# Gathers of a mixture-of-experts stage issued by two engines in turn instead of by one

## The chip, the cores and the metric

The kernel runs on 1 core of one Trainium2 chip. The metric is the device time of one execution in microseconds (us). The engines are TensorE (PE in the profile, with PEld for its weight loads), VectorE (DVE), ScalarE (ACT), GpSimd (POOL) and the sequencer SyncE (SP), which computes nothing and issues transfers. Sixteen DMA engines carry every transfer, whichever engine issued it.

## The reference, cut to what matters

```
x: (32, 256, 256), adj: (256, 256)
x = x + attention(layernorm(x), adj)           # 8 heads, masked softmax
h = layernorm(x)                               # 8192 rows of 256, in groups of 16 rows
grouped = h.reshape(B, S // 16, 16, D)
logits = einsum('bgtd,des->bgtes', grouped, controller) + tie
perm = (logits == max(logits over t))          # each of 64 experts picks one row of each group
inter = einsum('bgtesf,bgtes->bgesf', einsum('bgtd,desf->bgtesf', grouped, f1), perm)
inter2 = einsum('bgesf,esfd->bgesd', relu(inter), f2)
x = x + einsum('bgesd,bgtes->bgtd', inter2, perm)
```

The change is in the last two lines: the experts' products must come back from an order by expert to an order by group, and are then scattered to the rows.

## The kernel before, in words

Everything is float32. The first two thirds of the span are the attention, batch by batch. The rest is the mixture stage, of which this document speaks. It handles 64 tiles of 128 rows in 4 chunks (`CHUNKS`, `c` 0 to 3) of 16 tiles (`CT`). A chunk has two stages.

**Units.** Four units (`u` 0 to 3) of four tiles each (`t` 0 to 3). In program order TensorE does, for unit `u`: the transposes of the unit two ahead (L546), `select` of tile 0 (L650), the one-hot transposes of the next unit (L566), `select` of tile 1, the logits of the unit two ahead (L559), `select` of tiles 2 and 3. Each `select` leaves its result in four PSUM banks, which VectorE and ScalarE copy to `XS` (L246, half each), and the next `select` waits for both halves (`sel_dve`, `sel_act`). ScalarE's list for a unit is: copy of the transposes (`save_h2T`, L774, two copies), `save_selected` 0, copy of the one-hot matrix (`save_one_hot`, L779), `save_selected` 1, 2, 3. In chunk 3 the last two units have nothing ahead, so units 2 and 3 have no `save_h2T`, and unit 3 has no `save_one_hot`.

**Experts.** For 16 quads of experts: expand (L661), relu, contract (L682), a copy of the products to one of 5 slots of `stage` (L918 on ScalarE, L1246 on VectorE), and `move` (L325 on SP), a transfer of 512 KB from that slot to the DRAM tensor `scratch`. Each slot has its semaphore in `moved`.

**Gathers.** When all moves of chunk `c` have landed, 16 gathers (L335, on SP) bring `scratch` back by expert, one for each tile, 512 KB each, into the same 5 slots, now called `XR`: tile `i` goes to slot `i % 5`. They run beside the units of chunk `c + 1`, where TensorE does 8 scatters (L709) of two tiles each, between the selects: units 1, 2 and 3 have scatters 0 to 2, 3 to 5, and 6 and 7. The scatter after select 0 (and the one-hot transposes) comes first, then one after select 2, then one after select 3; unit 3 has only the first two. Scatter `s` needs tiles `2s` and `2s + 1` landed (`gathered`) and the result of scatter `s - 1` added by VectorE (`finish`, L1204). A gather of tile 5 or more waits until the scatter that read its slot is done:

```
                elif tile >= SLOTS:
                    sp.wait_ge(sc_ready, c * (CT // 2) + (tile - SLOTS) // 2 + 1)
```

So tiles 5 and 6 wait for scatter 0, 7 and 8 for scatter 1, 9 and 10 for scatter 2, 11 and 12 for scatter 3, 13 and 14 for scatter 4, and 15 for scatter 5. After the gathers SP stores the finished rows (L341, 8 transfers of 256 KB).

**Tail.** After the experts of chunk 3 there are no units. Four gathers of 2 MB (L356, on SP, into `XRlast`, four tiles each, semaphores `last_in`) are issued one behind the other, TensorE does two scatters (L695) for each that lands, VectorE adds them (L1204), and SP stores the rows (L341).

ScalarE issues transfers only at the very start of the kernel (weights and biases, L758 to L763); in the mixture stage it issues none.

Of the kernel before, what the change touches and what calls it, by code (L numbers as in the profile page):

```python
# [23 lines left out]
def gnn_moe_kernel(nc, x, adj, Wq, bq, Wk, bk, Wv, bv, Wo, bo, controller, f1, f2, out):  # L24
    B, N, D = x.shape
# [10 lines left out]
    CT = 16  # L36
    CHUNKS = TILES // CT
    UT = 4
    UNITS = CT // UT
    GPT = P // T  # L40
    CG = CT * GPT
    CP = CG // 2
    QUADS = ES // 4
    SLOTS = 5
# [23 lines left out]
    with ExitStack() as ctx:  # L68
# [200 lines left out]
        def products(q, hf):  # L269

            b = first_bank(q, hf)
            return stage[:, q % SLOTS, 2 * hf:2 * hf + 2, :], banks[:, b:b + 2, 0:D]

        def uses_of_slot(s):

            return (QUADS - s + SLOTS - 1) // SLOTS
# [10 lines left out]
        @block.sync  # L287
        def _(sp):
            def load_x(b, par):
                if in_loop(b) or (b - par) * 8 > 0:  # L290
                    sp.wait_ge(x_in[par], (b - par) * 8)
                sp.dma_start(xbatch(X1, b), xbatch(xt, b)).then_inc(x_in[par], 16)

            def stack_parts(b, par):

                sp.wait_ge(q_saved, b + 1)
                sp.wait_ge(k_saved, b + 1)
                for j in range(HPG):
                    src = parts[32 * j:32 * j + 32, par, :, :, :].rearrange("p s g n -> p s (g n)")
                    for r, chosen in enumerate((slice(0, 3, 2), slice(0, 4, 3), slice(1, 3, 1), slice(1, 4, 2))):  # L300
                        sp.dma_start(stack[32 * r:32 * r + 32, par, j, :, :].bitcast(F32), src[:, chosen, :].bitcast(F32))\  # L301
                            .then_inc(stacked[par][j // 2], 16)
            for b in range(6):
                load_x(b, b % 2)
                if b == 1:
                    sp.dma_start(adjs, adj.rearrange("(t p) k -> p t k", p=P)).then_inc(adj_in, 16)
            stack_parts(0, 0)
            stack_parts(1, 1)
            with sp.Fori(1, B // 2 - 2) as i:
                for par in range(2):  # L310
                    load_x(i * 2 + (4 + par), par)
                for par in range(2):
                    stack_parts(i * 2 + par, par)
            sp.dma_start(ctl[:, :, :], controller.rearrange("(t p) e s -> p t (e s)", p=P)).then_inc(ctl_in, 16)
            for b in range(B - 4, B):
                stack_parts(b, b % 2)
            sp.dma_start(f1s[:, :, :, :], f1.rearrange("(t p) e s f -> p t (e s) f", p=P)).then_inc(ffn_in, 16)
            sp.dma_start(f2s[:, :, :], f2.rearrange("e s f d -> (e s f) d").rearrange("(q p) d -> p q d", p=P))\
              .then_inc(ffn_in, 16)
            def move(c, q):  # L320

                n = c * QUADS + q
                sp.wait_ge(st_dve, n + 1)
                sp.wait_ge(st_act, n + 1)
                sp.dma_start(by_group(c, q), stage[:, q % SLOTS, :, :].rearrange("p j d -> p (j d)"))\  # L325
                    .then_inc(moved[q % SLOTS], 16)

            def gather(c, tile):

                if tile == 0:  # L330
                    for i, m in enumerate(moved):
                        sp.wait_ge(m, (c + 1) * uses_of_slot(i) * 16)
                elif tile >= SLOTS:
                    sp.wait_ge(sc_ready, c * (CT // 2) + (tile - SLOTS) // 2 + 1)
                sp.dma_start(XR[:, tile % SLOTS, :, :], by_expert(c, tile)).then_inc(gathered[tile % SLOTS], 16)  # L335

            def store(c, s):
                n = c * (CT // 2) + s
                sp.wait_ge(fin_done, n + 1)
                tiles = slice(2 * n, 2 * n + 2)  # L340
                sp.dma_start(ot[:, tiles, :], X1[:, tiles, :]).then_inc(out_done, 16)  # L341

            for c in range(CHUNKS - 1):
                for q in range(QUADS):
                    move(c, q)
                for tile in range(CT):
                    gather(c, tile)
                for s in range(CT // 2):
                    store(c, s)
            for q in range(QUADS):  # L350
                move(CHUNKS - 1, q)
            for i, m in enumerate(moved):
                sp.wait_ge(m, CHUNKS * uses_of_slot(i) * 16)
            for i in range(4):
                rows = slice((CHUNKS - 1) * CG + 4 * GPT * i, (CHUNKS - 1) * CG + 4 * GPT * (i + 1))
                sp.dma_start(XRlast[:, 4 * i:4 * i + 4, :, :].rearrange("p t j d -> p (t j) d"),  # L356
                             scratch[rows, :].rearrange("(c two) (e d) -> (two e) c d", two=2, d=D))\
                    .then_inc(last_in[i], 16)
            for s in range(CT // 2):
                store(CHUNKS - 1, s)  # L360
            sp.wait_ge(out_done, CHUNKS * (CT // 2) * 16)
# [394 lines left out]
        def _(act):  # L756
# [131 lines left out]
            def save_selected(c, u, t):  # L888
                act.wait_ge(sel_ready, c * CT + u * UT + t + 1)
                copy_selected(nc.scalar.copy, u * UT + t, 1).then_inc(sel_act, 1)  # L890

            def unit(c, u):
                n = c * UNITS + u
                ahead = n + AHEAD < CHUNKS * UNITS
                if ahead:
                    save_h2T(n + AHEAD)
                save_selected(c, u, 0)
                if n + 1 < CHUNKS * UNITS:
                    save_one_hot(n + 1)
                save_selected(c, u, 1)  # L900
                save_selected(c, u, 2)
                save_selected(c, u, 3)

            def experts(c):
                def save_inner(q):
                    act.wait_ge(in_ready, c * QUADS + q + 1)
                    if q >= INNERS:
                        act.wait_ge(f2_ready, (c * QUADS + q - INNERS) * 2 + 2)
                    nc.scalar.activation(inner[:, q % INNERS, :], bank[q % 2][:, 0:CG], ACT.Relu).then_inc(in_act, 1)
                save_inner(0)  # L910
                for q in range(QUADS):
                    if q + 1 < QUADS and (q + 1) % 2 == 0:
                        save_inner(q + 1)
                    act.wait_ge(f2_ready, (c * QUADS + q) * 2 + 2)
                    s = q % SLOTS
                    if landed(c, q) > 16:
                        act.wait_ge(moved[s], landed(c, q) - 16)
                    nc.scalar.copy(*products(q, 1)).then_inc(st_act, 1)  # L918

            for c in range(CHUNKS):  # L920
                for u in range(UNITS):
                    unit(c, u)
                experts(c)


        @block.vector
# [350 lines left out]
```

## Time and profile before

| | us |
|---|---|
| median of 3 timed runs | 808.16 (806.3 to 810.27) |
| profiled execution | 806.59 |
| its span | 804.8 |
| attention, up to the first unit | 0 to 544.3 |
| units of chunk 0 (no scatters) | 544.3 to 569.2 |
| units of chunk 1, with the gathers of chunk 0 | 591.2 to 627.7 |
| units of chunk 2, with the gathers of chunk 1 | 649.75 to 685.95 |
| units of chunk 3, with the gathers of chunk 2 | 708.0 to 743.6 |
| tail, from the last copy of products to the end | 766.4 to 804.8 |
| busy: PE 728.1, DVE 612.7, ACT 568.3, POOL 125.4 | |

Times within the kernel are microseconds from the start of the span. Between the unit stages lie the experts, 22 us each. The profiled execution is 1.8 us longer than its span and 1.6 us below the median of the timed runs.

### The profile page before, as it was taken

The numbers are of one execution on the slowest core, as the hardware profiler recorded it, in microseconds if no ns is written. First come the engines' busy times: TensorE is split into PE (matmuls) and PEld (weight loads), VectorE is DVE, ScalarE is ACT, GpSimd is POOL, SyncE is SP. The second block draws the span as 40 slices with busy tenths as digits, with TensorE's granted clock in tenths as the row PEclk, the third lists the DMA queues.
The fourth block names the chain that finished last, engine by engine and source line by source line (L and its number), as shares of the span: only waits on it lengthen the run. The fifth ranks groups of instructions, "written<-read, shape, count | busy, mean of one in ns | idle before, by whom it ended". The sixth has DMA issues, their size and how long they took to land.

```text
span 804.8 us, 22451 instructions
## 1 busy us (share of the span) xinstructions
PE 728.1 (90%) x7252; PEld 556.7 (69%) x7252; DVE 612.7 (76%) x2558; ACT 568.3 (71%) x1654; POOL 125.4 (16%) x125
## 2 busy tenths in 40 slices
PE   4789999999999999999999999897888988986925
PEld 3578888888888888888888888765554555553602
DVE  2588998998988989989989989777656656655612
ACT  3499899899999998998998999765553453442500
POOL 1100100000010010001001003436425225200000
PEclk9899999999999999999999999999999999999956
DMA  6476656756765765666567466650589889889889
GB/s 157 105 170 144 160 136 154 172 137 138 171 155 121 170 155 133 161 154 154 139 154 171 112 138 140 151 204 2 211 312 339 329 312 334 338 304 345 345 303 303
DMA packets 102197, 157.60 MB, mean 196 GB/s; under 512 B 12288, under 2 KB 65024, under 8 KB 101888
## 3 DMA queue, kind: packets, MB, share of 16 engines
q1 hardware_dynamic: 99968, 155.56, 67.7%
q10 hardware_dynamic: 2176, 1.31, 0.7%
q8 instruction: 35, 0.57, 0.3%
q14 instruction: 18, 0.15, 0.1%
HBM read 47.78 MB, written 41.94 MB: 111 GB/s over the span
## 4 chain that ended last, share of the span: by engine, by line
PE 71%; DMA 14%; SPq 6%; DVE 5%; issue 2%; ACT 1%; ACTq 0%; DVEq 0%
PE bank L501 13%; PE bank L453 12%; DMA stage<-scratch 7%; PE bank L515 7%; PE bank L488 7%; PE bank L475 6%; PE bank L682 6%; PE bank L538 6%; PE bank L661 5%; SPq L301 4%; DMA XRlast<-scratch 2%; PE bank L446 2%; DMA scratch<-stage 2%; PE bank L650 2%; PE bank L709 2%
## 5 line engine op out<-in xcount | busy, mean ns | idle before, releaser
L826 ACT ACTIVATE Ps<-Ps,nmax 128x256 f32<-128x256 f32 x512 | 255.3, 503 | 23.4 <-DVE nmax L1015 21.7
L1015 DVE CUSTOM_DVE_ANT_0 Ps<-bank,masks 128x256 f32<-128x256 f32 x512 | 199.3, 420 | 27.2 <-issue 25.4
L501 PE MATMUL bank<-ident,Ps 128*128 128x128 f32 x1024 | 145.6, 275 | 2.0 <-DVE PTs L1026 1.5
L501 PEld LDWEIGHTS bank<-ident,Ps 128*128 128x128 f32 x1024 | 115.8, 140 | 20.2 <-issue 12.4
L453 PE MATMUL bank<-hT,WT 128*128 128x256 f32 x512 | 125.2, 389 | 0.8 <-ACT hT L783 0.8
L488 PE MATMUL bank<-stack 128*128 128x256 f32 x512 | 118.0, 332 | 6.2 <-DMA stack<-parts 6.0
L382 POOL TENSOR_TENSOR X<-X,bob 128x512 f32 (+1 forms) x32 | 40.8, 1277 | 431.5 <-ACT hn L791 431.5
L453 PEld LDWEIGHTS bank<-hT,WT 128*128 128x128 f32 x512 | 95.6, 196 | 12.2 <-issue 1.1
L826 ACT ACTIVATION_READ_ACCUMULATOR Ps<-Ps,nmax 128x1 f32 x512 | 98.1, 192 | 0.0
L394 POOL TENSOR_SCALAR h<-X,mv,roots 128x256 f32<-128x256 f32 x64 | 80.1, 1263 | 113.5 <-PE bank L650 85.7
L1026 DVE COPY PTs<-bank 128x512 f32<-128x512 f32 x128 | 87.7, 685 | 4.9 <-PE bank L501 4.8
L488 PEld LDWEIGHTS bank<-stack 128*128 128x128 f32 x512 | 80.5, 191 | 14.1 <-issue 5.0
L246 ACT COPY XS<-bank 128x512 f32<-128x512 f32 x64 | 37.8, 590 | 59.9 <-PE bank L650 59.9
L835 ACT COPY PTs<-bank 128x512 f32<-128x512 f32 x128 | 73.9, 577 | 0.4 <-PE bank L501 0.4
L809 ACT ACTIVATE parts<-bank,few 128x256 fp32r<-128x256 f32 x128 | 53.7, 471 | 26.3 <-PE bank L453 24.3
L515 PE MATMUL bank<-PTs,Vs 128*32 128x256 f32 x1024 | 68.5, 385 | 0.0
L918 ACT COPY stage<-bank 128x512 f32<-128x512 f32 x64 | 37.5, 587 | 42.9 <-PE bank L682 42.9
L1001 DVE SCALAR_TENSOR_TENSOR parts<-bank,few,parts 128x256 fp32r<-128x256 f32 x128 | 58.0, 479 | 8.4 <-ACT parts L809 8.4
L246 DVE COPY XS<-bank 128x512 f32<-128x512 f32 x64 | 44.6, 697 | 26.0 <-PE bank L650 25.9
L475 PE MATMUL bank<-WT,hT 128*128 128x256 f32 x256 | 61.9, 385 | 2.0 <-DVE parts L1001 1.8
L1204 DVE TENSOR_TENSOR X<-X,bank 128x512 f32<-128x512 f32 x32 | 22.0, 688 | 54.7 <-PE bank L695 31.1
L1246 DVE COPY stage<-bank 128x512 f32<-128x512 f32 x64 | 43.9, 691 | 25.1 <-PE bank L682 25.1
(84 smaller groups left out, 1028.8 us busy)
## 6 DMA issues: line engine op xcount, KB each, us to landing
stack<-parts SPq DMA_DIRECT2D x512, 128.0 KB, 2.4
scratch<-stage SPq DMA_DIRECT2D x64, 512.0 KB, 4.0
stage<-scratch SPq DMA_DIRECT2D x48, 512.0 KB, 6.2
X<-in_x SPq DMA_DIRECT2D x32, 256.0 KB, 2.8
out<-X SPq DMA_DIRECT2D x32, 256.0 KB, 4.7
XRlast<-scratch SPq DMA_DIRECT2D x4, 2048.0 KB, 15.9
f1s<-in_L_ffn_f SPq DMA_DIRECT2D x1, 2048.0 KB, 8.0
f2s<-in_L_ffn_f SPq DMA_DIRECT2D x1, 2048.0 KB, 13.9
```

Of the source, the lines that this page charges most:

```text
L246: return copy(XS[:, :, :, first:first + 4].rearrange("p k e (j two) -> p k e j two", two=2), banks[:, 4 + 2 * hf:6 + 2 * hf, 0:2 * P].rear ...
L394: last = nc.gpsimd.tensor_scalar(h2[n % NORMS][:, t, :], xtile(tile), mv2[:, tile, 0:1], roots[:, 1, tile:tile + 1], ALU.subtract, ALU.mult)
L453: last = nc.tensor.matmul(m[:, g * N:g * N + N], WT[:, w, k, g * P:g * P + P], hT[:, k, :], start=(k == 0), stop=(k == KT - 1))
L475: last = nc.tensor.matmul(M[0][:, t * D:t * D + D], hT[:, k, t * P:t * P + P], WT[:, 2, k, :], start=(k == 0), stop=(k == KT - 1))
L488: last = nc.tensor.matmul(s_bank(n)[:, h * N:h * N + N], stack[:, par, j, 0, g * N + t * P:g * N + t * P + P], stack[:, par, j, 1, g * N:g ...
L501: last = nc.tensor.transpose(PTb[h % 2][:, k * N + t * P:k * N + t * P + P], Ps[:, pr % 2, t, h % 2, k * P:k * P + P], ident[:, :])
L515: last = nc.tensor.matmul(Ob[32 * j:32 * j + 32, g * N:g * N + N], Vs[:, par, k, h * DH:h * DH + DH], PTs[:, h, k * N:k * N + N], start=(k ...
L826: last = nc.scalar.activation(Ps[:, pr % 2, t, h, :], Ps[:, pr % 2, t, h, :], ACT.Exp, bias=nmax[:, pr % 2, t, h:h + 1], scale=-1.0, accum ...
L835: nc.scalar.copy(PTs[:, h, :], PTb[h % 2][:, :]).then_inc(pt_act, 1)
L1001: low = nc.vector.scalar_tensor_tensor(parts[:, par, 2 * which + 1, g, :], M[1 - which][:, g * N:g * N + N], (bqs, bks)[which][:, g:g + 1] ...
L1015: last = nc.vector.tensor_tensor_reduce(out=Ps[:, pr % 2, t, h, :], in0=s_bank(n)[:, h * N:h * N + N], in1=masks[:, t, :], scale=1.0, scal ...
L1026: nc.vector.tensor_copy(PTs[:, h, :], PTb[h % 2][:, :]).then_inc(pt_dve, 1)
```

## The change

Even tiles are gathered by SP as before. Odd tiles are gathered by ScalarE, on ScalarE's own queue, from within its list of the units: it waits for `moved` and issues tiles 1 and 3 in unit 0 behind `save_one_hot`, and issues the others ahead of certain `save_selected`, by a table. In the tail SP issues the first and the third 2 MB gather, and ScalarE the second and the fourth. The waits on `sc_ready` stay as they were for each tile.

```diff
@@ sync
-                for tile in range(CT):
+                for tile in range(0, CT, 2):
                     gather(c, tile)
...
-            for i in range(4):
-                rows = slice((CHUNKS - 1) * CG + 4 * GPT * i, (CHUNKS - 1) * CG + 4 * GPT * (i + 1))
-                sp.dma_start(XRlast[:, 4 * i:4 * i + 4, :, :].rearrange("p t j d -> p (t j) d"),
-                             scratch[rows, :].rearrange("(c two) (e d) -> (two e) c d", two=2, d=D))\
-                    .then_inc(last_in[i], 16)
+            for i in range(0, 4, 2):
+                sp.dma_start(*last_rows(i)).then_inc(last_in[i], 16)
@@ scalar, unit(c, u)
-                save_selected(c, u, 1)
-                save_selected(c, u, 2)
-                save_selected(c, u, 3)
+                if c > 0 and u == 0:
+                    for i, m in enumerate(moved):
+                        act.wait_ge(m, c * uses_of_slot(i) * 16)
+                    for tile in range(1, SLOTS, 2):
+                        gather(c - 1, tile)
+                after = {(1, 1): 5, (1, 3): 7, (2, 1): 9, (2, 2): 11, (2, 3): 13, (3, 1): 15}
+                for t in range(1, UT):
+                    if c > 0 and (u, t) in after:
+                        gather(c - 1, after[u, t])
+                    save_selected(c, u, t)
+
+            def gather(c, tile):
+
+                if tile >= SLOTS:
+                    act.wait_ge(sc_ready, c * (CT // 2) + (tile - SLOTS) // 2 + 1)
+                act.dma_start(XR[:, tile % SLOTS, :, :], by_expert(c, tile)).then_inc(gathered[tile % SLOTS], 16)
@@ scalar, after the last experts
+            for i, m in enumerate(moved):
+                act.wait_ge(m, CHUNKS * uses_of_slot(i) * 16)
+            for i in range(1, 4, 2):
+                act.dma_start(*last_rows(i)).then_inc(last_in[i], 16)
```

`last_rows(i)` returns the same pair of destination and source that the removed lines wrote out.

## Rows read from the trace of the kernel before

**Rows 1.** Page, the span in 40 slices: DMA share in tenths, and rate.

```profile
DMA  6476656756765765666567466650589889889889
GB/s 157 105 170 144 160 136 154 172 137 138 171 155 121 170 155 133 161 154 154 139 154 171 112 138 140 151 204 2 211 312 339 329 312 334 338 304 345 345 303 303
```

**Rows 2.** Windows, unit stages of chunks 2 and 3; PEclk is the granted clock.

```profile
core 0: us, PE busy (x) PEld busy (x) DVE busy (x) ACT busy (x) POOL busy (x), PEclk, DMA share, GB/s
649.75:685.95 36.20, 30.40 (x467) 18.50 (x465) 21.51 (x39) 15.84 (x29) 16.00 (x13) 1.00 0.94 314
708.00:743.60 35.60, 26.17 (x430) 15.33 (x428) 19.25 (x32) 13.46 (x24) 0.00 (x0) 1.00 0.95 318
```

**Rows 3.** Chain that ended last, units of chunk 2: start, duration, what.

```profile
660.65 6.67 DMA stage<-scratch
...
671.33 4.95 DMA stage<-scratch
...
677.03 6.50 DMA stage<-scratch
...
683.57 0.68 PE bank L709 x8
```

**Rows 4.** Windows, start of the gathers of chunk 1, then in full flow.

```profile
654.50:656.00 1.50, 0.69 (x20) 0.49 (x20) 1.25 (x3) 0.59 (x1) 0.00 (x0) 1.00 0.13 35
...
661.00:666.00 5.00, 3.82 (x72) 1.99 (x66) 3.04 (x6) 1.43 (x3) 0.74 (x2) 1.00 1.09 348
```

**Rows 5.** Gathers L335: all 48, then the first of chunk 1's alone.

```profile
L335 SPq DMA_DIRECT2D stage<-scratch x48: 354/502/937, 595.6 to 735.3; - x48
...
DMA to landing us min/median/max: 3.9/6.2/9.7
...
L335 SPq DMA_DIRECT2D stage<-scratch x1: 370/370/370, 654.6 to 654.6; - x1
...
DMA to landing us min/median/max: 3.9/3.9/3.9
```

**Rows 6.** Waits of SP from 650 to 686: total, times, longest.

```profile
SPq L335 <- PE bank L709: 15.2, 6, 3.5
```

**Rows 7.** Timeline of ACT: start, duration, instruction, idle before it.

```profile
652.31 0.62 ACT L779 COPY permR<-bank 128x512 f32<-128x512 f32 x1
653.37 0.59 ACT L246 COPY XS<-bank 128x512 f32<-128x512 f32 x1 [0.44 <-PE bank L650]
...
670.50 0.62 ACT L779 COPY permR<-bank 128x512 f32<-128x512 f32 x1
...
727.62 0.59 ACT L779 COPY permR<-bank 128x512 f32<-128x512 f32 x1
```

**Rows 8.** Timeline of PE, units of chunk 2.

```profile
658.72 0.64 PE L709 MATMUL bank<-stage,permT 128*32 128x256 f32 x8
...
664.38 0.64 PE L709 MATMUL bank<-stage,permT 128*32 128x256 f32 x8 [0.89 <-DMA stage<-scratch]
...
673.53 1.07 PE L709 MATMUL bank<-stage,permT 128*32 128x256 f32 x16
...
679.16 1.07 PE L709 MATMUL bank<-stage,permT 128*32 128x256 f32 x16
```

**Rows 9.** Transfers that ACT issues at the kernel's start (Wv, Wo).

```profile
L762 ACTq DMA_DIRECT2D PTs<-in_L_gnn_Wv x1: 493/493/493, 3.4 to 3.4; - x1
```

**Rows 10.** Tail, timeline of SP and PE.

```profile
770.65 14.20 SPq L356 DMA_DIRECT2D XRlast<-scratch  x4
...
797.98 3.46 PE L695 MATMUL bank<-XRlast,permT 128*32 128x256 f32 x32 [3.45 <-DMA XRlast<-scratch]
```

**Rows 11.** Tail, windows; then the stores L341 issued from 801 on.

```profile
785.00:798.00 13.00, 7.19 (x68) 2.77 (x68) 2.75 (x4) 0.00 (x0) 0.00 (x0) 0.63 1.09 352
...
L341 SPq DMA_DIRECT2D out<-X x1: 380/380/380, 802.2 to 802.2; - x1
...
DMA to landing us min/median/max: 2.1/2.1/2.1
```

More of the change, by code:

```diff
@@ L272, in products, with last_rows @@
             return stage[:, q % SLOTS, 2 * hf:2 * hf + 2, :], banks[:, b:b + 2, 0:D]
+        def last_rows(i):
+            rows = slice((CHUNKS - 1) * CG + 4 * GPT * i, (CHUNKS - 1) * CG + 4 * GPT * (i + 1))
+            return (XRlast[:, 4 * i:4 * i + 4, :, :].rearrange("p t j d -> p (t j) d"),
+                    scratch[rows, :].rearrange("(c two) (e d) -> (two e) c d", two=2, d=D))
         def uses_of_slot(s):
```

## The prediction

> **What bounds the kernel now.** I read the page's slices first, to see which part of the span lives on transfers: from the 30th slice on (584 us) the DMA engines are 8 or 9 tenths busy and move 303 to 345 GB/s [rows 1]. That is the mixture stage, and the change touches nothing before it. Then the windows of the unit stages, which are 36.2 and 35.6 us long with TensorE busy for 30.4 and 26.2 us at the full granted clock and the DMA share at 0.94 to 0.95 [rows 2]. So both are near their limit and neither is at it all the time. Next the chain that ended last, inside the units of chunk 2: transfer, scatter, transfer, scatter. It goes from gather to gather, and the last link is the scatter of tile 15 at 683.57 [rows 3]. This is what the reader is to see: the unit stage ends by the gathers, and a gather can only start when a scatter has freed its slot. A gather that is issued late is therefore late for its scatter, and that makes the next gather late.
>
> How much slack is there? In flow the engines move 348 GB/s with a share of 1.09 [rows 4], so a gather of 524,288 bytes takes 0.524288 / 0.348 = 1.5 us of all sixteen, and 16 take 24 us of the 29 between the first issue at 654.6 [rows 5] and 683.5. The first 1.5 us move nearly nothing [rows 4]. Alone, a gather lands 3.9 us after its issue; with others before it the median is 6.2 and the longest 9.7 [rows 5]. With five slots, three or four gathers must be in flight or the engines idle.
>
> **What the change takes away.** SP no longer issues 8 gathers of each chunk, at a median of 0.50 us [rows 5]: 4 us of SP's time for each chunk. But SP stood waiting for scatters 15.2 us in this stage [rows 6], so this time is hidden, except in the first burst, where tile 1 is issued 0.5 us sooner and tile 4 about 1 us. With the engines full soon after, that is worth 0 to 1 us for a chunk, and the next step takes it away. The Trainium skill (DMA: Bandwidth & Descriptors, "Issuing engines are not separate DMA queues") says that issuing from several engines only saves the sequencer's issue time, since all run on the same 16 engines. By that rule too the gain is the 4 us that stand beside a wait, so nothing.
>
> **What it adds, step by step, for chunk 2** (times are those of the profile before; "+" is the delay against it).
>
> 1. ScalarE's wait for `moved`. Its copy of the one-hot matrix ends at 652.31 + 0.62 = 652.93 and `save_selected` 1 starts at 653.37 [rows 7]. The moves have landed at 654.6, when SP issues [rows 5]. ScalarE now waits there until 654.6 and then issues tiles 1 and 3. The only issues by ScalarE in this trace take 0.49 us each [rows 9]. So the copy starts at about 655.65, 2.3 us later. Queued behind it is the whole list of unit 0, and `select` 2 waits for it: +2.1 on TensorE (0.2 was covered by the logits).
> 2. Scatter 0 was reached at 658.72 [rows 8], and its second tile only landed 1.2 us later. It is reached at 660.8 now with both tiles landed: its end moves by +1.4. Scatter 1 had waited for tile 3 until 664.38 [rows 8]; that wait swallows most of the rest: +0.5. Tiles 5 and 7 are issued right after their scatters, since the copies behind them need a later `select` anyway: they cost nothing. After unit 1: +0.5.
> 3. Tile 9 is free after scatter 2, at 668.1 (before) or 668.5 (now). But in ScalarE's list it stands behind two copies, a `save_selected` and the one-hot copy of unit 2, which ended at 670.50 + 0.62 = 671.1 [rows 7]. Now it goes out at 671.1 + 0.5 = 671.6, 3.5 us later. Tile 12 goes out on SP's queue at nearly the same time. Two gathers issued together share the engines: both land after 3.9 + 1.5 = 5.4 us. So tile 9 lands at 677.1. Scatter 4 ran from 673.53 [rows 8], and its second tile at about 674.1: +3.1. This is the largest single step.
> 4. Tile 11 goes out behind `save_selected` 1 of unit 2, 1.4 us after its slot is free: 673.2, landed at 678.8. Scatter 5's second tile started at 676.3 (the transfer from 671.33 ended then) [rows 3]: +2.6, within the delay of step 3.
> 5. Tiles 13 and 14 leave together behind scatter 4, at 678.0, landed at 683.5. Scatter 6 ran from 679.16 [rows 8], its second tile at 679.7: +3.8.
> 6. Tile 15 is again behind `save_h2T`, `save_selected` 0 and `save_one_hot`, now of unit 3. It was issued at 677.0 [rows 3]; scatter 5 now ends at 680.0, the three copies at about 683.0, and it lands 5.4 to 6.5 us later (6.5 is what it took before, among the stores [rows 3]): 688.4 to 689.5. The scatter of tile 15 started at 683.57: +5.4, taken between the two.
>
> Chunk 2's units therefore become 5.4 us longer. Bounds: if the late gathers land as one alone does (3.9), 3.5 us; if every late one takes 6.2 to 6.5 us, as in the flow before, and each of three turns adds that 1 us, 8.4 us. No row shows two queues with gathers in both, so I keep both ends. The units of chunk 1 have the same list and the same order: 5.4 again (its ScalarE wait is 0.4 us shorter, but that is swallowed in step 2). In chunk 3 units 2 and 3 have no `save_h2T`, and unit 3 has no one-hot copy: the one-hot copy of unit 2 ends at 727.62 + 0.59 = 728.2 [rows 7], 1.9 us and not 3.5 behind the old issue, and tile 15 is 1.3 us late. That gives +2.3 (bounds 1 and 4).
>
> The experts' stages, 22 us each, have nothing of the change in them and begin only when all selects are done; they shift and don't absorb anything. Sum of the units: 5.4 + 5.4 + 2.3 = 13.1, bounds 8 and 21.
>
> **The tail.** Four gathers of 2 MB begin at 770.65 and the last lands at 797.98, at 352 GB/s and a share of 1.09 [rows 10, 11]. This is bytes over rate: 8.39 MB / 0.352 = 23.8 us, and a second queue moves no byte less. What changes is the order. One queue delivered them one by one, so six of the eight scatters were done when the last landed, and 3.46 us of scatters (two of them, at half clock) were left [rows 10]. With two queues shared evenly, the first and second land together at about 785, and the third and fourth together at 797, 1 us sooner than before since no store stands in front. Then four scatters are left, 4 x 1.75 = 7.0 us instead of 3.5. Net: -1.0 + 3.5 = +2.5. The last addition (0.7) and store, landed after 2.1 us [rows 11], are unchanged. Bounds: -1 (SP's queue is served first) and +3.5. The Trainium skill (DMA: Bandwidth & Descriptors, "Queues, rings and completion order") has each DMA engine go round robin between queues, which is the even sharing. No row of this trace shows it.
>
> **Sum.** 13.1 + 2.5 = 15.6 us. Against the profiled execution, 806.6 + 15.6 = 822.2; its span would be 820.4. The profiled execution is 1.6 us below the median of the timed runs, 808.2, so the time is 808.2 + 15.6, rounded to 823. The bounds of the terms are 8 - 1 = 7 and 21 + 3.5 = 24.5: 815 to 833.
>
> **Rivals.**
>
> *Two queues carry more than one (faster).* If the 348 GB/s of the flow is a limit of one queue and not of the engines, and two reach the 400, then 24 us of gathers become 21 in each of three stages and 23.8 become 21 in the tail: -3 each where transfers bind, -12 in all, against delays of ScalarE that shrink with the shorter landings to about 6 us: 802. It decides from about 375 GB/s in the flow on. Against it: the share is already 1.09, so no engine has a gap to fill [rows 4, 11], and late issues leave them idle whatever the rate is. Chance 0.08.
>
> *Nothing (same).* Transfers bind, ScalarE is busy for only half of the stage, and the late issues lie under gathers that are still on the way: 808. For it: a DMA share of 0.94 over the stage [rows 2]. Against it: this needs the engines to have work for the 3.5 us that tile 9 is late, and there are only tiles 7, 8 and 10, 4.5 us of which 2 have gone by when scatter 2 ends. The rule of the Trainium skill quoted above would by itself give this time, as it knows of no list on the issuing engine. Chance 0.07.
>
> *A small loss.* Only the wait for `moved` and the tail count: 3 x 0.5 + 2.5 and a little: 812 to 815. Chance 0.08.
>
> *The issue itself blocks ScalarE.* The fifth gather of a burst took SP 0.94 us to issue [rows 5], and the four of the tail 14.2 us [rows 10]. If ScalarE's issues take that 0.94 or longer, each of 8 adds 0.5 us to the copies behind it: up to +4 for a chunk, 835. Against it: never more than two or three gathers are in ScalarE's queue, and the long issues come with four or more. Chance 0.07.
>
> The forecast itself, 815 to 833, has 0.70.
>
> **How the numbers follow.** This kernel's runs differ by half a per cent (806.3 to 810.3), so 0.5%, 4 us, is what can be told from no change. Faster is the first rival alone, 0.08. Same is the second, 0.07. Slower is the rest, 0.70 + 0.08 + 0.07 = 0.85. The range from 811 to 833 leaves out the first two rivals and the last, 0.2 or so.
>
> **What would show each step.** In the profile after: in unit 0 of chunks 1 to 3 a gap of some 2 us on ScalarE before its second copy, ended by the moves. The issue of tile 9 about 3 us after scatter 2, and scatter 4 waiting for a transfer, which it didn't before. Scatter 7 waiting longer than the 0.4 us of before. The DMA share of the unit stages falling from 0.94 towards 0.82 (the same bytes in a stage 5 us longer). Chunk 3's stage growing by less than half of the others. In the tail, the first scatter at 785 instead of 779 and four scatters back to back at the end. Wrong would be: unit stages of 36 us as before; a flow above 370 GB/s; scatters of the tail that start at 779.

## The result, and the profile after

The changed kernel takes 834.16 us (median of 4 runs, 831.02 to 834.8) against 807.23 us for the kernel before on the same chip: a ratio of 1.0315, 95% interval 1.0287 to 1.0344. That is 27 us slower, where 15.6 had been forecast. Its profiled execution took 834.8 us, with a span of 833.0, 28.2 more than before. The end of the range, 833, is 1 us under the median.

First the windows of the three unit stages after, and of the experts behind the first, in the columns of [rows 2].

```profile
core 0: us, PE busy (x) PEld busy (x) DVE busy (x) ACT busy (x) POOL busy (x), PEclk, DMA share, GB/s
591.44:636.36 44.92, 34.63 (x467) 21.27 (x465) 21.50 (x39) 16.03 (x29) 16.00 (x13) 0.89 0.78 257
659.69:704.40 44.71, 34.18 (x468) 20.77 (x467) 21.61 (x39) 16.03 (x29) 15.75 (x13) 0.89 0.78 260
728.00:771.10 43.10, 30.25 (x429) 17.73 (x429) 19.28 (x32) 13.65 (x24) 0.00 (x0) 0.88 0.81 266
636.36:659.69 23.33, 23.02 (x384) 14.04 (x385) 13.41 (x26) 11.02 (x23) 4.13 (x4) 0.93 0.80 319
```

The stages were 36.5, 36.2 and 35.6 us long and are 44.9, 44.7 and 43.1: +8.4, +8.5 and +7.5, together 24.4 of the 28.2 us. The DMA share fell from 0.94 to 0.78 and the rate from 314 to 257 GB/s. So the sixteen engines carry the same bytes with more idle time. The last row shows something else: the experts' stage, in which no line was changed, takes 23.3 us where it took 22.05, with the granted clock at 0.93. The stage behind chunk 2 is 1.5 us longer too. Not all of this is the change's: the experts of chunk 0, which run before the first changed transfer, also took 23.3 us at a clock of 0.93 in this execution (and in that of wait_only below).

The timeline of ScalarE in chunk 2 shows the new issues; [rows 7] has the same copies before.

```profile
662.26 0.62 ACT L782 COPY permR<-bank 128x512 f32<-128x512 f32 x1
664.71 1.02 ACTq L918 DMA_DIRECT2D stage<-scratch  x2
665.76 0.59 ACT L246 COPY XS<-bank 128x512 f32<-128x512 f32 x1 [2.89 <-issue]
...
674.83 0.46 ACTq L918 DMA_DIRECT2D stage<-scratch  x1
...
683.14 0.37 ACTq L918 DMA_DIRECT2D stage<-scratch  x1
683.33 0.62 ACT L782 COPY permR<-bank 128x512 f32<-128x512 f32 x1
```

ScalarE stands from 662.9 to 664.7 waiting for the moves, spends 1.02 us on the issues of tiles 1 and 3, and only then makes the copy that `select` 2 waits for. Tile 9 goes out at 683.14, that is 2.3 us after scatter 2 freed its slot (at 680.83). Now TensorE in the same stage, beside [rows 8]:

```profile
666.50 0.73 PE L653 MATMUL bank<-permR,h 32*128 32x128 f32 x16 [2.22 <-ACT XS L246]
668.02 1.24 PE L653 MATMUL bank<-permR,h 32*128 32x128 f32 x16 [0.80 <-DVE XS L246]
669.19 1.97 PE L549 MATMUL bank<-ident,h 128*128 128x128 f32 x8
...
673.30 1.45 PE L712 MATMUL bank<-stage,permT 128*32 128x256 f32 x16
...
680.19 0.64 PE L712 MATMUL bank<-stage,permT 128*32 128x256 f32 x8 [0.66 <-DMA stage<-scratch]
...
687.88 0.64 PE L712 MATMUL bank<-stage,permT 128*32 128x256 f32 x8 [0.86 <-DMA stage<-scratch]
...
690.82 0.64 PE L712 MATMUL bank<-stage,permT 128*32 128x256 f32 x8 [0.85 <-DMA stage<-scratch]
...
695.71 0.64 PE L712 MATMUL bank<-stage,permT 128*32 128x256 f32 x8 [1.42 <-DMA stage<-scratch]
...
701.34 1.06 PE L712 MATMUL bank<-stage,permT 128*32 128x256 f32 x8 [2.10 <-DMA stage<-scratch]
```

And a window of the same stage, in the columns of the first:

```profile
668.00:672.00 4.00, 3.98 (x40) 3.42 (x40) 1.73 (x4) 1.39 (x3) 2.61 (x3) 0.50 1.08 356
```

Read it from the top. TensorE waits 2.22 us for ScalarE's copy, and soon after, the same `select` takes 1.24 us and not 0.73, and the transposes 1.97 and not 1.1. The window from 668 to 672 shows why: a granted clock of 0.50, so 1.2 GHz and not 2.4, behind the wait. Scatters 2, 4, 5, 6 and 7 each wait for their second tile, 0.66, 0.86, 0.85, 1.42 and 2.10 us; scatter 3 does not. Before, scatters 4 and 6 had no such wait, 5 and 7 waited 0.28 and 0.44, and scatters 0 and 1, which now wait for nothing, had waited 0.59 and 0.89. Against the start of the stage, TensorE is 2.9 us late at the end of unit 1, 3.8 at the second tile of scatter 4, 6.0 at that of scatter 6, 7.8 at that of scatter 7, and 8.5 at the end.

The tail, timeline of SP, ScalarE and TensorE after, beside [rows 10]:

```profile
798.18 2.62 SPq L361 DMA_DIRECT2D XRlast<-scratch  x2
798.19 6.64 ACTq L943 DMA_DIRECT2D XRlast<-scratch  x2
811.09 3.38 PE L698 MATMUL bank<-XRlast,permT 128*32 128x256 f32 x32 [17.86 <-DMA XRlast<-scratch]
...
824.32 5.31 PE L698 MATMUL bank<-XRlast,permT 128*32 128x256 f32 x64 [7.72 <-DMA XRlast<-scratch]
```

The first gather lands 12.9 us after its issue, where it took 8.3 before, and four scatters stand back to back at the end. The last two of them are those of ScalarE's second gather, which landed 29.2 us after the first issue; in the kernel before the last gather landed after 27.3. From the first issue to the end of the span it is 34.8 us, against 34.15 before: +0.7.

### The profile page after: what moved, and what is told of

Read it like the earlier page. It is cut to its first block, busy times and chain, and to the rows that moved or that the text cites. A ratio compares the mean times of both kernels' runs of the same rounds, so it can differ in the third digit from the quotient of the medians.

```text
span 833.0 us, 22459 instructions
## 1 busy us (share of the span) xinstructions
PE 739.7 (89%) x7252; PEld 565.7 (68%) x7252; DVE 610.8 (73%) x2558; ACT 569.4 (68%) x1654; POOL 125.2 (15%) x125
## 4 chain that ended last, share of the span: by engine, by line
PE 73%; DMA 14%; DVE 5%; SPq 4%; issue 2%; ACT 2%; ACTq 1%; DVEq 0%
PE bank L504 13%; PE bank L456 11%; PE bank L518 7%; DMA stage<-scratch 7%; PE bank L491 7%; PE bank L478 6%; PE bank L541 6%; PE bank L685 6%; PE bank L664 5%; SPq L307 4%; DMA XRlast<-scratch 3%; PE bank L653 3%; PE bank L449 2%; DMA scratch<-stage 2%; PE bank L712 2%
## 5 line engine op out<-in xcount | busy, mean ns | idle before, releaser
L504 PEld LDWEIGHTS bank<-ident,Ps 128*128 128x128 f32 x1024 | 115.8, 140 | 20.3 <-issue 12.3
L653 PE MATMUL bank<-permR,h 32*128 32x128 f32 x1024 | 50.7, 316 | 17.5 <-ACT XS L246 9.2
```

The lines of the kernel that those rows point to most:

```text
L504: last = nc.tensor.transpose(PTb[h % 2][:, k * N + t * P:k * N + t * P + P], Ps[:, pr % 2, t, h % 2, k * P:k * P + P], ident[:, :])
L653: last = nc.tensor.matmul(bank[4 + j][:, k * P:k * P + P], h2[n % NORMS][r, t, k * P:k * P + P], permR[r, n % 2, t * P:t * P + P], start=T ...
```

## The experiments

Each kernel ran beside the kernel before on the same chip. Ratios are against that. Where microseconds are given, they are the ratio less one, times 807. All experiments on the units have the tail as before.

### The parts by themselves

**units_only**: the tail's edit undone.

```diff
-            for i in range(0, 4, 2):
+            for i in range(4):
                 sp.dma_start(*last_rows(i)).then_inc(last_in[i], 16)
...
-            for i in range(1, 4, 2):
-                act.dma_start(*last_rows(i)).then_inc(last_in[i], 16)
```

> The change in the units as it is, the tail as before. Theory A (late issues and the fall of the granted clock that follows each wait, both in the units): the trace of after has 24.3 us of its 28 in the three unit stages and 2.5 in the experts behind them, so +26 to +28 us on the kernel before. Theory B (the sum of the prediction, units 13, tail 2.5, and the rest in how two queues share the engines, tail included): +13 to +20.

Measured: ratio 1.0278 (1.0243 to 1.0313), +22 us. Between the two bands; the interval reaches down into theory B's and stays just short of theory A's.

**tail_only**: the reverse, the units as before and the two-queue tail.

```diff
-                for tile in range(0, CT, 2):
+                for tile in range(CT):
                     gather(c, tile)
...
-                    for tile in range(1, SLOTS, 2):
-                        gather(c - 1, tile)
-                after = {(1, 1): 5, (1, 3): 7, (2, 1): 9, (2, 2): 11, (2, 3): 13, (3, 1): 15}
+                after = {}
```

(The wait for `moved` in unit 0 is left out as well.)

> The two-queue tail alone, units as before. Theory A: in the trace of after the tail from the landing of the last move to the end is 34.8 us against 34.15, so 0 to +1.5 us. Theory B (prediction): +2.5, since four scatters at half clock follow the last landing instead of two.

Measured: ratio 1.0022 (1.0002 to 1.0043), +1.8 us, with 0.2 to 3.5 in the interval: both theories fit. Nearly all of the loss is in the units.

**first_on_sync**: tiles 1 and 3 on SP, no wait for the moves on ScalarE.

```diff
-                for tile in range(0, CT, 2):
-                    gather(c, tile)
+                for tile in range(CT):
+                    if tile % 2 == 0 or tile < SLOTS:
+                        gather(c, tile)
...
-                if c > 0 and u == 0:
-                    for i, m in enumerate(moved):
-                        act.wait_ge(m, c * uses_of_slot(i) * 16)
-                    for tile in range(1, SLOTS, 2):
-                        gather(c - 1, tile)
```

> As units_only, but tiles 1 and 3 stay on SP and ScalarE does not wait for the moves. Theory A: the start of each unit stage, up to the first scatter, gives back its 4.4 us, and the clock no longer falls there: of +27 some +12 to +15 stay, from the late tiles 9, 11 and 15. Theory B (prediction: this step is worth 0.5 us of 5.4 a chunk, as the next wait swallows it): only 1.5 us less than units_only.

Measured: ratio 1.0305 (1.0252 to 1.0359), +25 us, no better than units_only. Theory A falls here: the most visible wait of the changed profile, with its slow clock behind it, costs nothing that can be measured. Theory B's 1.5 us less was not seen either, but lies within the intervals. The first scatter stands 9.0 us into the stage, as in the kernel before, and not at 12.3 to 13.7 as in units_only, and this lead is lost at scatter 2. The timeline of TensorE in this kernel, chunk 1, shows where:

```profile
608.34 0.64 PE L713 MATMUL bank<-stage,permT 128*32 128x256 f32 x8 [0.28 <-DMA stage<-scratch]
611.25 1.08 PE L713 MATMUL bank<-stage,permT 128*32 128x256 f32 x8 [2.27 <-DMA stage<-scratch]
612.26 1.97 PE L550 MATMUL bank<-ident,h 128*128 128x128 f32 x8
```

Tile 5 was issued by ScalarE at once behind scatter 0, at 603.1, and landed 8.1 us later. In the kernel before it took 6.5. So a tile issued in time still lands late, and the slow clock now follows this wait. Removing the first wait let another one come out, so this run doesn't show by itself that the first is cheap; the next one does.

**wait_only**: the kernel before, with only the wait.

```diff
+                if c > 0 and u == 0:
+                    for i, m in enumerate(moved):
+                        act.wait_ge(m, c * uses_of_slot(i) * 16)
```

> The kernel before with only the wait of ScalarE for the moves in unit 0, at the place where the change has it; SP issues all gathers. ScalarE's copy comes 1.2 to 1.4 us later. Theory A: if this gap alone lets the granted clock fall, +4 us a chunk, +9 to +13; if the gap is too short for that, under +3. Theory B: +0 to +1.5, since the next wait for a gather swallows it.

Measured: ratio 1.0022 (1.0000 to 1.0045), +1.8 us. The wait does almost nothing by itself, as first_on_sync says from the other side.

### The order in which a pair lands

A scatter frees two slots, for tiles 2s + 5 and 2s + 6. The odd one is needed one scatter earlier. One queue delivers it first; two queues share the engines and deliver both at about the time of the second (tiles 6 and 5 after 4.7 and 5.3 us in chunk 2 of the changed kernel, the one that is needed later even first). **swapped_pairs** takes away the second queue and keeps only the wrong order: SP issues all 16, each pair reversed.

```diff
-                for tile in range(CT):
+                for tile in (0, 1, 2, 3, 4, 6, 5, 8, 7, 10, 9, 12, 11, 14, 13, 15):
                     gather(c, tile)
```

> One queue, SP issues everything as before, but each pair of tiles that one scatter frees goes out in the other order (6 before 5, 8 before 7, ... 14 before 13). Theory C (a new one, from the traces: the two tiles of a pair, issued together on two queues, share the engines and both land at the time of the second, and the first is the one that the next scatter but one needs): the tile that is needed first lands 1.5 us later, five times a chunk, as with two queues, so with neither a second queue nor a late issue +4 to +10 us. Theory D (late issues of 9, 11 and 15 behind ScalarE's list are the cost): this has none, +0 to +2.

Measured: ratio 1.0139 (1.0109 to 1.0170), +11 us. One queue, no late issue, no work on ScalarE. This is at the upper end of theory C's 4 to 10 or above it, and theory D, which gave 0 to 2, falls as the whole account. The timeline of TensorE in its chunk 2, scatter 2 and the transposes behind it:

```profile
672.52 0.64 PE L709 MATMUL bank<-stage,permT 128*32 128x256 f32 x8 [0.28 <-DMA stage<-scratch]
675.43 0.64 PE L709 MATMUL bank<-stage,permT 128*32 128x256 f32 x8 [2.27 <-DMA stage<-scratch]
676.00 1.74 PE L546 MATMUL bank<-ident,h 128*128 128x128 f32 x8
677.67 1.24 PE L650 MATMUL bank<-permR,h 32*128 32x128 f32 x16
```

Scatter 2's second tile, tile 5, is waited for 2.27 us; before it was 0.76. Landing one place later in a queue of 1.5 us a place is enough. The other chunks have the same wait (2.24 and 2.29). Behind it TensorE runs at its lower clock (transposes 1.74 us and not 1.09, `select` 1.24 and not 0.73), so the delay of 1.5 us has become 3.0 when scatter 3 starts. What this run measures is the wrong order together with the slow clock that its waits bring on.

**first_sync_early** and **pairs_together** have two queues and no late issue. Tiles 0 to 4 are on SP in both and tile 15 on ScalarE, at the head of unit 3. The first splits pairs by parity; its edit against first_on_sync:

```diff
+                if c > 0 and u > 1:
+                    gather(c - 1, (9, 15)[u - 2])
                 if ahead:
                     save_h2T(n + AHEAD)
...
-                after = {(1, 1): 5, (1, 3): 7, (2, 1): 9, (2, 2): 11, (2, 3): 13, (3, 1): 15}
+                after = {(1, 1): 5, (1, 3): 7, (2, 1): 11, (2, 3): 13}
```

The second keeps each pair on one queue; against first_sync_early:

```diff
-                    if tile % 2 == 0 or tile < SLOTS:
+                    if tile not in (7, 8, 11, 12, 15):
...
-                if c > 0 and u > 1:
-                    gather(c - 1, (9, 15)[u - 2])
+                if c > 0 and u > 2:
+                    gather(c - 1, 15)
...
-                after = {(1, 1): 5, (1, 3): 7, (2, 1): 11, (2, 3): 13}
+                after = {(1, 3): (7, 8), (2, 1): (11, 12)}
...
-                        gather(c - 1, after[u, t])
+                        for tile in after[u, t]:
+                            gather(c - 1, tile)
```

> Two queues by even and odd tiles from tile 5 on, ScalarE's issues moved to the head of units 2 and 3 and ahead of its first wait, so none is late; tiles 0 to 4 on SP. Theory C: pairs are still split, so most of the +27 stays, +10 to +25. Theory D: gone, +0 to +3.

> Two queues, but the two tiles of a pair stay on one queue in their order: SP has 0 to 6, 9, 10, 13, 14, and ScalarE 7, 8, 11, 12 and 15, each issued where ScalarE waits for that scatter anyway, so nothing is late. Theory C: no pair is shared out, +0 to +3 us. Theory D: nothing is late, +0 to +3 as well. A third, E (two queues as such, or SP's stores running ahead of tile 15): +5 or more here.

Measured: first_sync_early 1.0218 (1.0159 to 1.0277), +18 us; pairs_together 1.0114 (1.0071 to 1.0157), +9 us. The point estimates give 7 us for the late issues (first_on_sync less first_sync_early) and 8 for splitting the pairs; the intervals of the first two kernels overlap and those of the last two only just part (1.0159 and 1.0157), so these two sizes are rough. (The medians alone would give 10.6 us for the late issues, which is the 10 in a later expectation.) And 9 us remain with neither, which was theory E.

### Tile 15 and the stores

**pairs_15_on_sync**: pairs_together with tile 15 on SP, ahead of SP's stores.

```diff
-                    if tile not in (7, 8, 11, 12, 15):
+                    if tile not in (7, 8, 11, 12):
...
-                if c > 0 and u > 2:
-                    gather(c - 1, 15)
```

> As pairs_together, but tile 15 too goes out on SP, ahead of SP's stores: ScalarE has 7, 8, 11 and 12 only. Theory E1 (SP's stores overtake tile 15 when that stands on the other queue; it landed 8 us after its issue there): +1 to +4 instead of the +10 of pairs_together. Theory E2 (two queues as such cost, wherever the tiles go): still +7 or more.

Measured: ratio 1.0002 (0.9970 to 1.0034). The 9 us are gone, and with them all of the change's cost: two queues as such, with four of sixteen tiles on ScalarE's and whole pairs, cost nothing and gain nothing. The windows of a stretch in which both queues carry gathers, from 668 to 674 in its chunk 2, with the bytes of each queue (q1 is SP's, q10 ScalarE's), and of the same place in the kernel before:

```profile
668.00:674.00 6.00, 5.79 (x81) 3.65 (x85) 3.19 (x6) 2.64 (x5) 3.63 (x3) 1.00 1.05 339
q1 hardware_dynamic: 1035, 1.03, 52.4%
q10 hardware_dynamic: 1000, 0.99, 51.3%
...
667.00:673.00 6.00, 5.63 (x80) 3.54 (x84) 3.19 (x7) 2.64 (x5) 3.88 (x4) 1.00 1.04 341
```

Two queues moved 339 GB/s and one moved 341.

The chain that ended last, chunk 2's tile 15, in pairs_together:

```profile
678.25 9.12 DMA stage<-scratch
687.37 0.04 issue
687.42 0.84 PE bank L713 x8
```

and in pairs_15_on_sync:

```profile
677.71 6.15 DMA stage<-scratch
683.85 0.04 issue
683.90 0.68 PE bank L713 x8
```

The issue is 0.5 us apart, the landing 3.5 (counted from the start of each stage, 1.1 and 4.1). In the three chunks tile 15 took 8.0, 9.1 and 8.1 us to land in pairs_together, and 6.6, 6.1 and 5.1 in pairs_15_on_sync. The difference is what SP does meanwhile. In pairs_together SP's list has no tile 15, so it goes on to the stores at once (timeline of SP):

```profile
676.37 0.91 SPq L341 DMA_DIRECT2D stage<-scratch  x2
677.32 12.08 SPq L347 DMA_DIRECT2D out<-X  x8
```

The first stores start at 677.32, ahead of tile 15; in pairs_15_on_sync at 678.11, behind it. The unit stages of pairs_together are 37.4, 40.2 and 39.3 us long, those of pairs_15_on_sync 36.8, 35.6 and 35.4, which is the 9 us. Shown is that the place of tile 15 costs them; that it is the stores is read here from the order of the issues and the late landing. The next run bears it out.

**stores_held** tries the same on the change itself: units_only, with the stores held until tile 15 is out.

```diff
+                sp.wait_ge(sc_ready, c * (CT // 2) + 7)
                 for s in range(CT // 2):
                     store(c, s)
```

> units_only with SP's stores of a chunk held until scatter 6 is done, so that tiles 13, 14 and 15 are on their way before the first store. Theory E1: tile 15 lands sooner by the time of the five stores ahead of it, 3 to 4 us, and 13 and 14 by 1 to 2: +10 to +16 instead of the +24 of units_only. If the late issue of 15 itself is what counts: +20 or more.

Measured: ratio 1.0241 (1.0177 to 1.0305), +19 us: 3 less than units_only, less than the intervals can tell. Theory E1 was right about tile 15 and wrong about what it is worth. Tile 15's issue and its landing, chunk 2:

```profile
688.60 0.37 ACTq L919 DMA_DIRECT2D stage<-scratch  x1
DMA to landing us min/median/max: 3.9/3.9/3.9
```

With the first store 2 to 3 us behind it, tile 15 landed 3.9, 3.9 and 4.0 us after its issue in the three chunks; in units_only, which differs by the held stores alone, it took 4.4, 7.2 and 7.2. So the stores do make it late, by some 3 us in two of three chunks. But scatter 7 then waits for nothing, and the stage is ended by what lies before it. In chunk 2 scatter 6 waited 1.69 us for tile 13, which took 7.9 us to land although no store was under way; the granted clock fell behind that wait, and the stage took 43.8 us. The stages were 39.7, 43.8 and 41.9 us against 42.3, 42.1 and 43.1 in units_only. Why tile 13 took so long is open, and so is how much of the change's own loss the stores make.

**early_places**: units_only, with the issues moved to where the slots come free; the first wait and tiles 1 and 3 stay on ScalarE.

```diff
+                if c > 0 and u > 1:
+                    gather(c - 1, (9, 15)[u - 2])
                 if ahead:
                     save_h2T(n + AHEAD)
...
-                after = {(1, 1): 5, (1, 3): 7, (2, 1): 9, (2, 2): 11, (2, 3): 13, (3, 1): 15}
+                after = {(1, 1): 5, (1, 3): 7, (2, 1): 11, (2, 3): 13}
```

> units_only with ScalarE's issues moved to where each slot comes free: 9 at the head of unit 2, 11 ahead of save_selected 1, 15 at the head of unit 3; the wait for the moves and tiles 1 and 3 stay on ScalarE. Late issues, as first_on_sync less first_sync_early gave them, are worth 10 us: +13 to +17 instead of +24. If the first wait matters most: +20 or more.

Measured: ratio 1.0234 (1.0174 to 1.0294), +19 us, 3.5 less than units_only, with intervals that overlap. Between the two bands. Together with the 7 us above, the late issues are worth 3 to 7 us by the ratios, less than the order and the stores by the point estimates. Issued early, tile 15 took 7.7, 8.8 and 7.7 us to land, so it was still held up among the stores. Early issues and held stores together were not run.

### The clock

**filled** is units_only with transposes whose result is never read, where TensorE waits; **before_filled** is the kernel before with the same transposes.

```diff
                 if ahead:
                     logits(n + AHEAD)
+                if c > 0 and u == 0:
+                    for _ in range(14):
+                        nc.tensor.transpose(bank[3][:, 0:P], ident[:, :], ident[:, :])
...
+                    if tt == 1 and s in (2, 5, 7):
+                        for _ in range(12):
+                            nc.tensor.transpose(bank[3][:, D:D + P], ident[:, :], ident[:, :])
                     pe.wait_ge(gathered[tile % SLOTS], landed(c, tile))
```

> units_only with transposes whose result nobody reads, put where TensorE waits: 14 in unit 0 behind the logits, and 12 between the two tiles of scatters 2, 5 and 7. They keep TensorE busy where it would stand for 1.3 to 2 us. If the granted clock accounts for half of the loss (busy time of TensorE in the three unit stages and the experts behind them is 15 us above before's): +12 to +18 in place of +24. If it only lengthens work that the transfers hide: +22 or more.

> The kernel before with the filling transposes of filled, the control for these: the clock is full there anyway. If they stand under waits, +0 to +3 us; filled less this is the change's cost with a full clock. Theory of the clock as half of the loss: the difference is 12 to 15 us. Theory that transfers hide the slow clock: the difference is 19 us or more.

Measured: filled 1.0274 (1.0253 to 1.0295), the same as units_only; before_filled 1.0085 (1.0054 to 1.0117), +7 us. The windows of the three unit stages, of units_only and then of filled:

```profile
594.77:637.10 42.33, 33.18 (x467) 20.99 (x465) 21.49 (x39) 16.02 (x29) 15.97 (x13) 0.92 0.83 273
659.16:701.28 42.12, 32.24 (x467) 19.70 (x465) 21.50 (x39) 15.96 (x29) 15.97 (x13) 0.96 0.82 273
724.61:767.67 43.06, 32.41 (x431) 18.98 (x429) 19.32 (x32) 13.63 (x24) 0.00 (x0) 0.80 0.81 267
...
589.23:633.09 43.86, 37.92 (x516) 24.32 (x514) 21.50 (x39) 15.84 (x29) 16.00 (x13) 0.96 0.80 263
655.16:699.29 44.13, 37.79 (x517) 25.11 (x515) 21.51 (x39) 15.99 (x29) 16.00 (x13) 0.96 0.80 262
721.36:767.47 46.11, 35.79 (x481) 22.76 (x479) 19.29 (x32) 13.46 (x24) 0.00 (x0) 0.89 0.76 249
```

In filled the granted clock is 0.96, 0.96 and 0.89, against 0.92, 0.96 and 0.80 in units_only: the filling gave back only a part, and in chunk 2 nothing. The stages did not get shorter, with the DMA share at 0.80, 0.80 and 0.76. By itself this looks as if the transfers hid the slow clock. The control says otherwise: the filling costs 7 us in the kernel before, where 0 to 3 had been expected, and some of that may be in filled too. filled less before_filled is 15 us (12 to 18, an estimate from the two intervals), at the edge of the 12 to 15 that stood for the clock as half of the loss, and not the 19 or more of transfers that hide it. If the filling costs nothing in filled, the clock that it gave back was worth nothing; if it costs the same 7 us there, it was worth 7. So the part of the slow clock that was given back is worth 0 to 7 us of the 22, by point estimates; the rest was not tested.

One stage bounds it from the other side. Chunk 2 of units_only ran at 0.96 and still took 42.1 us, against 36.2 before: most of the loss is there with TensorE nearly at its full clock.

## Why the prediction was right in direction and short in size

Right: the kernel is slower, by waits on gathers, in the units, with idle DMA engines and no gain from the second queue. The term that failed is the sum of the units, 13.1 us with bounds 8 and 21. units_only measured 22 (20 to 25 by its interval), at the upper bound or above it. It was sized from ScalarE's first wait and the late issues; left out were the order in which a pair lands, the stores that reach tile 15 while it is under way, and the fall of the granted clock behind each wait of some 2 us.

- *Step 1, ScalarE's wait for the moves:* +2.1 on TensorE forecast, 2.22 us of wait measured. Right.
- *Step 2, its delay swallowed by the waits for tiles 1 and 3:* at the end of unit 1 the delay was forecast as +0.5; in the trace it was +2.9 (680.76 - 659.69 against 667.93 - 649.75), since the clock fell behind the wait, which I had not counted. But most of that delay was swallowed later: at the second tile of scatter 4 the trace has +3.8 for the forecast's +3.1, wait_only puts the whole first wait at 1.8 us (0 to 3.6), and first_on_sync, without it, was no faster. The step's conclusion held, its path did not.
- *Step 3, tile 9 issued late:* 3.5 us forecast, 2.3 measured (683.14 against the end of scatter 2 at 680.83), 0.8 of the difference because the transfer went out at 683.14 and not behind the one-hot copy ahead of it, which ended at 683.95. It landed after 4.7 us and not 5.4. The late issues together are worth 3 to 7 us in three chunks; I had made them nearly the whole of 13.1.
- *What was missing first:* the order within a pair. I had the even sharing of two queues and used it only for latency, 5.4 us for both. That tile 2s + 5 is needed one scatter before tile 2s + 6, and that one queue gives it that lead for nothing, was in the kernel's text. Step 2 even says of tiles 5 and 7 that "they cost nothing". swapped_pairs puts this at 11 us by itself (with the slow clock behind its waits), and first_sync_early less pairs_together at about 8.
- *What was missing second:* SP's stores. Step 6 gave tile 15 a latency of 5.4 to 6.5, the 6.5 read from a trace where it stood ahead of the stores. In chunk 2 it took 7.5 (issued 693.77, landed 701.3). With no other fault this order costs 9 us (pairs_together less pairs_15_on_sync), and with the stores held the same transfer takes 3.9. The stores reach tile 13 too, for which step 5 had 5.5: it took 7.1, and the delay at scatter 6 was 6.0 and not 3.8.
- *Chunk 3:* +2.3 forecast, +7.5 measured. The reason given, fewer copies ahead of ScalarE's issues, concerns only the late issues. Split pairs and stores act there as in the others, and that stage had the most waits for gathers already.
- *The experts' stages:* "don't absorb anything", true, but two of them came out 1.3 and 1.5 us longer, at a granted clock of 0.93 and 0.92, a slow stretch that began at the end of the units before them. How much of this is the change's is open, as the experts of chunk 0 had the same 1.2 us ahead of it.
- *The tail:* +2.5 forecast, +0.7 in the trace and +1.8 (0.2 to 3.5) by tail_only. Four scatters stood at the end as forecast, but the gathers did not land in twos: 12.9 and 16.4 us after the first issue, then 26.1 and 29.2. The last landed 1.9 us later than before, where 1 us sooner was forecast. Against that, two of the four scatters ran while it was on its way, and the last two took 1.9 us together (granted clock 1.00 from 827.7 on), so all four took 5.3 us and not 7.0. The small sum is two misses that nearly cancel.
- *Rivals:* two queues do not carry more than one: 356 GB/s from 668 to 672 in the changed kernel and 339 in pairs_15_on_sync with both queues loaded, against 341 to 357 with one. The changed kernel does reach 380 GB/s, from 694 to 700, when stores run beside the last gathers, but so does the kernel before at that place (380 from 682 to 685.5). The 375 that the prediction took as the mark was too low for such a stretch. ScalarE's issues in the units took 0.37 to 0.54 us, so they did not block it. The rule of the Trainium skill (DMA: Bandwidth & Descriptors, "Issuing engines are not separate DMA queues") holds in pairs_15_on_sync. It says that the transfers interleave, and the larger part of the 22 us came from what this did to the order in which they landed.

The sizes do not add: 3 to 7 for late issues, 8 to 11 for split pairs, 9 for the stores and 2 for the first wait make 22 to 29, and fixing the stores alone in the changed kernel gave back 3. Whichever of them ends last in a chunk hides the others. That the late issues are worth anything rests on intervals that overlap. The slow clock is not a further term beside these: it follows the waits that the first wait, the order and the stores make.

No version beat the kernel before; pairs_15_on_sync equals it.

## What to carry to other kernels

One queue is also an order: whoever splits it must ask, for each pair of transfers that come free together, which is needed first, and what the first engine's list goes on to when a transfer is taken out of it. Here, with the DMA engines nearly full, a transfer that landed one place too late, or beside stores that nobody waited for, cost more than the issue time that a second engine saved. And the longest wait in the profile after a change need not be its cost: here removing it changed nothing, because another wait took its place.

## What the runs showed of the hardware

- Two gathers of 512 KB issued in the same moment on two queues, with nothing else under way, landed after 4.7 and 5.3 us (SP's and ScalarE's, both at 674.8 in chunk 2 after); on one queue, in the kernel before, the first landed 3.9 us after its issue [rows 5] and the second, issued 0.4 us later, 5.3 us after the first's issue.
- In the tail two queues of 2 MB gathers were shared roughly evenly, SP's ahead: 2.16 MB against 1.63 from 800 to 811, and SP's landed 12.9 and 26.1 us after the start, ScalarE's 16.4 and 29.2. The Trainium skill (DMA: Bandwidth & Descriptors, "Queues, rings and completion order") has the engines go round robin between queues; the sharing agrees with that in the main, and SP's lead is not explained here.
- A transfer alone on a second queue did not pass those of the same size on the first: tile 5, alone on ScalarE's queue in first_on_sync (chunk 1), landed 8.1 us after its issue, at 611.2, behind the four gathers on SP's (tiles 2, 3, 4 and 6, the last issued with it and landed at 610.5).
- ScalarE's sequencer issued tile 9 at 683.14 although the one-hot copy ahead of it in its list began at 683.33: so an issue need not wait until the engine has begun the instructions ahead of it.
- An issue by ScalarE that began 5 ns behind one by SP took 0.46 us (tile 5 at 674.83), and alone 0.37 (tile 9 at 683.14).
